# Value and output weight multiplied together ahead of the key loop, loads reordered, second key weight split inside the loop

## What is computed

```python
# first part: q is the normalised x, k = v = ctx_1024
qp = einsum('bsd,ed->bse', q, Wq) + bq
kp = einsum('bsd,ed->bse', k, Wk) + bk
vp = einsum('bsd,ed->bse', v, Wv) + bv
scores = einsum('bqd,bkd->bqk', qp, kp) * scale
attn = softmax(scores, axis=-1)
out = einsum('bqk,bkd->bqd', attn, vp)
x = x + einsum('bsd,ed->bse', out, Wo) + bo
# second part, its start
qkv = layernorm(x) @ W_qkv
q, k, v = split(qkv, 3)      # rmsnorm and relu on q and k follow
```

## Time and profile before

| | |
|---|---|
| median of 3 runs | 548.07 us (547.96 to 549.03) |
| the profiled execution | 548.39 us, span 546.3 us |
| TensorE products busy | 538.7 us, 99% of the span |
| TensorE weight loads busy | 451.8 us, 83% |
| VectorE, ScalarE, GpSimd busy | 345.9, 256.8, 197.4 us |
| first q product, first score, first product of Wv | 10.33, 34.61, 390.66 us |

### The profile page before, as it was taken

The page is one execution under the profiler, slowest core; times in us unless marked ns, Lnnn a source line. Parts: engine busy times, 40 slices in busy tenths (PEclk is TensorE's granted clock), DMA queues, the critical chain, the costliest instruction groups (busy, mean ns, idle before and its releaser), DMA issues.

```text
span 546.3 us, 7076 instructions
## 1 busy us (share of the span) xinstructions
PE 538.7 (99%) x2612; PEld 451.8 (83%) x2612; DVE 345.9 (63%) x574; ACT 256.8 (47%) x421; POOL 197.4 (36%) x125
## 2 busy tenths in 40 slices
PE   8999999999999999999999999999999999999997
PEld 7998887788888888888888888888878888888886
DVE  5745555866477655557986546998536226638757
ACT  5624346745445545454455435575355452562210
POOL 3860421312211143232212433385099709800000
PEclk9999999999999999999999999999999999999999
DMA  8602432342232224222223123423302203300002
GB/s 326 245 28 77 158 112 74 126 148 78 86 145 78 77 79 146 86 77 78 91 91 127 40 77 128 180 81 123 145 0 62 93 1 119 113 1 1 0 2 77
DMA packets 14002, 51.61 MB, mean 94 GB/s; under 512 B 1680, under 2 KB 1680, under 8 KB 13072
## 3 DMA queue, kind: packets, MB, share of 16 engines
q1 hardware_dynamic: 13968, 51.16, 26.3%
HBM read 50.11 MB, written 1.05 MB: 94 GB/s over the span
## 4 chain that ended last, share of the span: by engine, by line
PE 95%; ACT 2%; DVE 2%; issue 1%; DMA 1%; DVEq 0%
PE bank L1195 28%; PE bank L1267 11%; PE bank L1269 11%; PE bank L1268 11%; PE bank L1256 10%; PE bank L1258 10%; PE bank L1257 10%; PE bank L1185 1%; PE bank L1423 1%; DMA xs<-x 1%; PE bank L1432 0%; ACT xn L548 0%; DVE xT_l L806 0%; PE bank L1295 0%; PE bank L1551 0%
## 5 line engine op out<-in xcount | busy, mean ns | idle before, releaser
L457 POOL TENSOR_TENSOR cn_l<-raw_n,cn_h 128x1024 fp32r<-128x1024 f32 x32 | 80.1, 2502 | 207.9 <-ACT cn_h L587 207.9
L886 DVE TENSOR_TENSOR top<-top,bank 128x512 f32<-128x512 f32 x60 | 41.2, 687 | 101.1 <-ACT ring L611 100.8
L1256 PE MATMUL bank<-qk_h,ct_h 128*128 128x512 f32 x256 | 100.1, 391 | 1.1 <-DVE top L886 1.1
L1267 PE MATMUL bank<-ph,cn_h 128*128 128x512 f32 x256 | 100.4, 392 | 0.0
L1269 PE MATMUL bank<-ph,cn_l 128*128 128x512 f32 x256 | 99.7, 390 | 0.0
L1258 PE MATMUL bank<-qk_h,ct_l 128*128 128x512 f32 x256 | 99.7, 389 | 0.0
L1268 PE MATMUL bank<-pl,cn_h 128*128 128x512 f32 x256 | 99.7, 389 | 0.0
L1257 PE MATMUL bank<-qk_l,ct_h 128*128 128x512 f32 x256 | 99.7, 389 | 0.0
L611 ACT COPY ring<-bank 128x512 f32<-128x512 f32 x64 | 37.5, 586 | 75.1 <-PE bank L1258 75.1
L621 ACT ACTIVATE ph<-ring 128x512 fp32r<-128x512 f32 x64 | 40.4, 632 | 65.1 <-PE bank L1269 47.4
L913 DVE TENSOR_TENSOR ring<-ring,shift_b 128x512 f32<-128x512 f32 x64 | 60.4, 949 | 2.0 <-ACT shift_b L632 2.0
(11 more groups left out here) (213 smaller groups left out, 900.2 us busy)
## 6 DMA issues: line engine op xcount, KB each, us to landing
raw_t<-ctx_t SPq DMA_DIRECT2D x32, 512.0 KB, 4.2
raw_n<-ctx_n SPq DMA_DIRECT2D x32, 512.0 KB, 3.3
...
```

Of the source, the lines that this page charges most:

```text
L457: pool.tensor_tensor(cn[p % CNB][1][:], raw_n[p % 2][:], cn[p % CNB][0][:].bitcast(F32), ALU.subtract).then_inc(cnl_ready, 1)
L1256: pe.matmul(bank[:, dst, :], ct[i // 2 % 2][0][:, c, keys], qk[0][:, c, :], start=(c == 0), stop=False)
L1267: pe.matmul(bank[:, c, :], keys[0][:, q % 2, d], ph[q % PB][:], start=first, stop=False)
```

## The change

TensorE now computes wvo = Wv and Wo multiplied together (`fold_part`, 48 products of 512 columns) at the start, while x is loaded and normalised; its four inner chunks e follow one another over four banks, and the transposes of x stand between them. Wv, Wo and x come first on SyncE's queue, in pieces of 256 KB, and then Wq. ScalarE and VectorE split Wv and the first chunk of Wo, GpSimd the other three chunks. q and qk are computed in full width (96 products of 512 columns in place of 192 of 256). A small activation at the start (`root_table`) stands ahead of ScalarE's first cast.

In the tail the value product and the spreading of the inverse denominators are gone: the unscaled accumulator is split, one product with wvo gives y (48 products), and the scale is applied as a factor per row where y is added to x. The bias bv is carried through Wo by GpSimd (`bv_wo`, seven operations) and one plain f32 product behind score 6, and is added to bo (`y_bias`), which GpSimd adds to x as it did with bo.

The key weight of the second part (w2 k) has memory of its own now, is loaded at p = 24 and split by GpSimd behind its work on context pieces 17 and 18; the others stay in the tail, with the casts of w2 v moved on ScalarE between the applies of the LayerNorm. The one-column products for the key bias move from behind score 0 to behind score 4.

The diff, cut to its core (declarations, semaphores, memory places, the full-width q and qk evacuations, the removed value product and the split of w2 k, which is that of the other w2 weights, are left out):

```diff
-W2_ORDER = ("k", "out", "q", "v")
-W2_HIGH = {51: ("k", 0), 53: ("k", 1), 55: ("out", 0), 57: ("out", 1)}
-W2_LOW_ORDER = ("k", "q", "v", "out")
+W2_ORDER = ("out", "q", "v")
+W2_HIGH = {55: ("out", 0), 57: ("out", 1)}
+W2_LOW_ORDER = ("q", "v", "out")
+K2_SPLIT = {17: 0, 18: 1}
...
-            for t in range(0, TT, 2):
-                for n in range(t, t + 2):
-                    sp.dma_start(xs[:, n, :], x[n]).then_inc(x_loaded[n], 16)
-                for e in range(t, t + 2):
-                    sp.dma_start(wq_raw[:, e, :], wq_t[e]).then_inc(wq_loaded[e], 16)
+            def load_weights(e):
+                sp.dma_start(wv_raw[:, e, :], wv_in[e]).then_inc(wv_loaded[e], 16)
+                sp.dma_start(wo_raw[:, e, :], wo_t[e]).then_inc(wo_loaded[e], 16)
+            def load_x(t):
+                sp.dma_start(xs[:, t, :], x[t]).then_inc(x_loaded[t], 16)
+            load_weights(0)
+            load_x(0)
+            load_weights(1)
+            load_x(1)
+            load_x(2)
+            load_weights(2)
+            load_x(3)
+            load_weights(3)
+            for e in range(C):
+                sp.dma_start(wq_raw[:, e, :], wq_t[e]).then_inc(wq_loaded[e], 16)
...
-            sp.dma_start(wvo_raw[:], wv_t).then_inc(wv_loaded, 16)
...
-                if p == 6:
-                    sp.wait_ge(wvo_ready, 2)
-                    sp.dma_start(wvo_raw[:], wo_t).then_inc(wo_loaded, 16)
-                if p == NP + 3:
-                    sp.wait_ge(ctl_ready, NP)
+                if p == 24:
+                    sp.wait_ge(bo_added, TT)
                     sp.dma_start(w2_raw["k"][:], wqkv_in[1]).then_inc(w2_loaded["k"], 16)
...
+            def split_wo(e):
+                pool.wait_ge(wo_loaded[e], 16)
+                pool.tensor_copy(wo[0][:, e, :], wo_raw[:, e, :]).then_inc(wo_high, 1)
+                pool.wait_ge(wo_high, e)
+                pool.tensor_tensor(wo[1][:, e, :], wo_raw[:, e, :], wo[0][:, e, :].bitcast(F32), ALU.subtract).then_inc(wo_ready, 1)
+            pool.memset(ones[:], 1.0).then_inc(ones_ready, 1)
+            for e in range(1, C):
+                split_wo(e)
...
+            pool.wait_ge(wv_ready, C)
+            pool.wait_ge(ctl_ready, 2)
+            for e in range(C):
+                dst = bv_term if e else bv_wo
+                if e == 0:
+                    pool.wait_ge(wo_loaded[0], 16)
+                else:
+                    pool.wait_ge(bv_step, 2 * e - 1)
+                pool.tensor_scalar(dst[:], wo_raw[:, e, :], col("bv", e), None, ALU.mult).then_inc(bv_step, 1)
+                if e:
+                    pool.wait_ge(bv_step, 2 * e)
+                    pool.tensor_tensor(bv_wo[:], bv_wo[:], bv_term[:], ALU.add).then_inc(bv_step, 1)
             pool.wait_ge(xn_ready, TT)
+            pool.wait_ge(y_bias_ready, 1)
             for t in range(TT):
-                pool.tensor_tensor(xs[:, t, :], xs[:, t, :], row("bo"), ALU.add).then_inc(bo_added, 1)
-            pool.wait_ge(qk_psum, 2 * C)
...
+                if p in K2_SPLIT:
+                    split_k2(K2_SPLIT[p])
...
+            act.wait_ge(ones_ready, 1)
+            act.activation(root_table[:], ones[:], ACT.Sqrt)
+            high_wv(0)
+            act.wait_ge(wo_loaded[0], 16)
+            act.copy(wo[0][:, 0, :], wo_raw[:, 0, :]).then_inc(wo0_high, 1)
+            high_wv(1)
             std_of(0)
             apply_of(0)
+            std_of(1)
...
-            act.wait_ge(inv_psum, 1)
-            act.wait_ge(acc_scaled, (NSB - 1) * C)
-            act.copy(alpha_b[:], bank[:, MISC, :]).then_inc(invb_ready, 1)
             for c in range(C):
-                act.wait_ge(xn_ready, TT + c + 1)
+                act.wait_ge(acc_added, (NSB - 1) * C + c + 1)
                 act.copy(onT[0][:, c, :], acc[:, c, :]).then_inc(xh_ready, 1)
             for h in range(2):
                 high_w2("q", h)
-            for e in range(C):
-                act.wait_ge(v_psum, e + 1)
-                act.activation(vT[0][:, e, :], bank[:, V_BANKS[e], :], ACT.Identity,
-                               bias=col("bv", e)).then_inc(vTh_ready, 1)
-            for h in range(2):
-                high_w2("v", h)
             for t in range(TT):
                 if t >= 2:
                     high_xT(2 * TT + t - 2, X1_BANKS)
                 std_of(TT + t)
                 apply_of(TT + t)
-            act.wait_ge(w2_ready, 2 * 3)
+                if t % 2 == 0:
+                    high_w2("v", t // 2)
+            act.wait_ge(w2_ready, 2 * 2)
...
+            low_wv(0)
+            dve.wait_ge(wo0_high, 1)
+            dve.tensor_tensor(wo[1][:, 0, :], wo_raw[:, 0, :], wo[0][:, 0, :].bitcast(F32), ALU.subtract).then_inc(wo0_ready, 1)
+            low_wv(1)
             first_stats(0)
             ln_scale(0)
             first_stats(1)
             ln_scale(1)
+            low_wv(2)
             first_stats(2)
+            ln_scale(2)
             low_xT(0, XT_BANKS)
-            ln_scale(2)
+            first_stats(3)
+            low_wv(3)
+            ln_scale(3)
             low_xT(1, XT_BANKS)
-            first_stats(3)
-            ln_scale(3)
             low_xT(2, XT_BANKS)
...
+            for c in range(C):
+                dve.wait_ge(wvoh_ready, c + 1)
+                dve.tensor_tensor(wvo[1][:, c, :], bank[:, WVO_BANKS[c], :], wvo[0][:, c, :].bitcast(F32),
+                                  ALU.subtract).then_inc(wvol_ready, 1)
+            for n in range(2):
+                low_ct(n)
+            for c in range(C):
+                dve.wait_ge(qkh_ready, c + 1)
+                dve.tensor_tensor(qk[1][:, c, :], bank[:, Q_BANKS[c], :], qk[0][:, c, :].bitcast(F32),
+                                  ALU.subtract).then_inc(qkl_ready, 1)
...
+                if s == 1:
+                    sum_key_terms()
+                if s == 8:
+                    biases()
...
-                if c == 0:
-                    dve.wait_ge(invb_ready, 1)
-                dve.wait_ge(acc_added, (NSB - 1) * C + c + 1)
-                dve.tensor_tensor(acc[:, c, :], acc[:, c, :], alpha_b[:], ALU.mult).then_inc(xn_ready, 1)
                 if c > 0:
                     low_on(c - 1)
             low_on(C - 1)
-            for e in range(C):
-                dve.wait_ge(vTh_ready, e + 1)
-                dve.scalar_tensor_tensor(out=vT[1][:, e, :], in0=bank[:, V_BANKS[e], :],
-                                         scalar=col("bv", e), in1=vT[0][:, e, :].bitcast(F32), op0=ALU.add,
-                                         op1=ALU.subtract).then_inc(vTl_ready, 1)
+            dve.wait_ge(inv_ready, 1)
             dve.wait_ge(bo_added, TT)
             for t in range(TT):
                 dve.wait_ge(y_psum, t + 1)
-                dve.tensor_tensor(xs[:, t, :], xs[:, t, :], bank[:, Y_BANKS[t], :], ALU.add).then_inc(x1_ready, 1)
+                dve.scalar_tensor_tensor(out=xs[:, t, :], in0=bank[:, Y_BANKS[t], :], scalar=inv_den[:, t:t + 1],
+                                         in1=xs[:, t, :], op0=ALU.mult, op1=ALU.add).then_inc(x1_ready, 1)
...
+            def fold_part(e, c):
+                ins = project(WVO_BANKS[c], [cut(wv, e, c * P, (c + 1) * P)], [cut(wo, e, 0, D)], starts=(e == 0),
+                              stops=(e == C - 1))
+                if e == C - 1:
+                    ins.then_inc(wvo_psum, 1)
+            transposed_at = {(1, 2): 0, (2, 0): 1, (2, 2): 2, (3, 1): 3}
+            for e in range(C):
+                pe.wait_ge(wv_ready, e + 1)
+                if e == 0:
+                    pe.wait_ge(wo0_ready, 1)
+                else:
+                    pe.wait_ge(wo_ready, e)
+                for c in range(C):
+                    fold_part(e, c)
+                    if (e, c) in transposed_at:
+                        transpose_x(transposed_at[e, c])
+            pe.wait_ge(xl_ready, TT)
+            for e in range(C):
                 pe.wait_ge(wq_ready, e + 1)
-                part = slice(h * HALF, (h + 1) * HALF)
-                project(Q_BANKS[h][e], [cut(wq, e, c * P, (c + 1) * P) for c in range(C)],
-                        [cut(xT, c, part.start, part.stop) for c in range(C)], cols=part).then_inc(q_psum, 1)
-            transpose_x(0)
-            warm(KEEP_WARM)
-            transpose_x(1)
-            warm(KEEP_WARM)
-            q_half(0, 0)
-            transpose_x(2)
-            q_half(0, 1)
-            transpose_x(3)
-            q_half(0, 2)
-            q_half(0, 3)
-            for e in range(C):
-                q_half(1, e)
+                project(Q_BANKS[e], [cut(wq, e, c * P, (c + 1) * P) for c in range(C)],
+                        [cut(xT, c, 0, T) for c in range(C)]).then_inc(q_psum, 1)
             pe.wait_ge(wk_ready, 1)
...
+            for c in range(C):
+                for e in range(C):
+                    if c == 0:
+                        pe.wait_ge(qTl_ready, e + 1)
+                    if e == 0:
```

(33 more changed lines are left out.)

237 lines of the change are left out of this document (105 added, 132 removed).

## The result

The changed kernel takes **544.88 us** (median of 4 runs, 544.64 to 545.55) against 548.43 for the kernel before in the same set (547.96 to 549.03). The ratio is 0.9939, with a 95% interval of 0.9928 to 0.9951, so 3.3 us less, where 3.3 us less was forecast; the two medians themselves lie 3.55 us apart. The profiled execution took 544.86 us, span 543.1. A second set gave 544.99 us and 0.9938 (0.9926 to 0.9951), with medians 3.25 us apart.

The account below looks back on a forecast made before the run. TensorE, busy 538.7 of 546.3 us, was taken to bound the kernel. Start +7.3, bias product +1.0, score 4 +0.1 and tail -11.7 sum to -3.3 us: 544.8 for the median, range 542.6 to 547.7.

Parts of the forecast that it names:

- The start, +7.3: Start of kernel to first score: 41.9 us against 34.61, so 7.3 us later; bounds +6.0 to +9.5.
- VectorE's list: At the start: VectorE's subtractions, statistics and scales, 11.8 us without a wait from 6.7, set when q starts.
- The 1.2 us "between": At the start: VectorE waits about 1.2 us for x^T of tile 1 and 2 and for ScalarE's casts between.
- The collision term of 0.4: At the start: VectorE loses about 0.4 us behind GpSimd's wo subtractions, through shared SBUF interfaces.
- Full width, -1.2: q and qk at the start: 96 products of 512 columns take 1.2 us less than 192 halves.
- The kept-warm products "worth nothing": Old start: the kept-warm product groups between transposes lay inside waits, so dropping them costs nothing.
- rival D: Start: TensorE falls back to 1.2 GHz or has not risen, products take 0.45 us; 550.2 us, slower; chance 0.08.
- The bias product, +1.0: In the loop: the new plain f32 512-column bv row product costs 1.0 us; bounds 0.2 to 1.1.
- Score 4, +0.1: In the loop: score 4 waits for VectorE's qb sum, ct_l and peak 2, 0.1 us; bounds 0 to 0.5.
- Wk2's split, 0: In the loop: GpSimd's 6.9 us of work behind cn 17 and 18 costs 0; bounds 0 to 1.5.
- rival E: In the loop: splitting Wk2 there starves VectorE, 2 x 1.5 us lost, 547.8 us; chance 0.04.
- The tail, -11.7: Tail: first y finished 11.5 us sooner, then 0.2 less to the third projection's end; bounds -10.6 to -12.3.

Follow-up runs that it names:

- the split of the bias: Changed kernel with the plain f32 bias product made two f32r products, split by GpSimd: 546.26 us; with GpSimd's extra operations held back: 544.30 us.

## Why the prediction was right, point by point

**The start, +7.3: right in size, but the chain was another, by a hair.** The first q product came at 19.99 (20.1 forecast) and the first score at 41.87 (41.9). The sum took VectorE's list for the longest. In the changed kernel the chain that ended last was GpSimd's wo_l of part 1 and, behind it, TensorE's own order; VectorE's list ended only 0.05 us earlier, as the kernel without that wait shows (q at 19.94). So the list's length was forecast well, and that a second chain ended at the same moment, so that the number held, is luck. Nor does the list reach q without a break, as the sum had it. Its last shift is made at 16.54, and xn of tile 3 is ready at 17.6; but the transposes come at 17.98, when TensorE's order reaches them, and then a cast and a subtraction follow. VectorE was idle before the last two:

```profile
18.63 1.31 DVE L845 TENSOR_TENSOR xT_l<-bank,xT_h 128x512 fp32r<-128x512 f32 x2 [1.28 <-ACT xT_h L586]
```

The 1.2 us "between" in the sum stood for this, by luck of size. The collision term of 0.4 was a wv subtraction of 1.27 us for 0.69, 0.6.

**GpSimd's wo_l of part 1**: forecast at 8.7 to 9.2, came at 9.46, since wo1 landed at 7.1 and not 6.7 and the cast took 0.93 and not 0.6; TensorE waited 0.64, not 0.0 to 0.5. It stands on the chain that ended last, and yet only 0.05 us hung on it.

**Full width, -1.2**: right (2.0 with the wait that halves bring in the new order).

**The kept-warm products "worth nothing"**: wrong. They lay inside waits by TensorE's idle time, and yet held its clock; without them the old start loses 1.8 us. The sum did not fall with this, since it measured before's start as it was, and in the changed kernel the granted clock read 1.00 from 6 to 18 us, with fold products 0.23 apart from the second on, so rival D did not come. That the fold's products do what the kept-warm ones did is the likely reason; no kernel tested it. But the argument against D was weak. It rested on gaps of 0.4 to 0.8 us among busy stretches, and in the old start without the kept-warm products the clock fell around gaps of 1.25 and 1.43 us, with four transposes between them. The "gaps far longer than those I find" were no more than that, in a stretch that held little else.

**The bias product, +1.0**: measured 0.86. Between the product at 61.69 and that at 63.01 lie 1.32 us, of which two pitches of 0.23 are ordinary. **Score 4, +0.1**: no wait. VectorE's running maximum for it was ready at 52.46 and score 4 began at 52.75, so the margin was at most 0.3 us where 0.05 was forecast: small all the same, as the split of the bias showed. **GpSimd's bias chain** ran from 38.2 to 48.9 ("over by 48"): its multiplications took 1.57 us, just above the 0.6 to 1.5 taken. With 2 us more it would have stood over the chain to score 4, and nothing in the sum had a term for that.

**Wk2's split, 0**: right, rival E did not come. The split could as well have stayed in the tail.

**The tail, -11.7**: Y at 403.16 gives -11.5 as forecast. The 0.3 before the first k is there (Y + 7.49 for 7.35) but not for the reason named: not the cast of w2 v, but the statistics of tile 1, in line ahead of the cast of xT 0. The 0.4 before the first v is there (Y + 13.40 for 13.3) and for the reason named. The "-0.2" came out as 0.0, from these two sizes. GpSimd's slack at the last v projection was forecast as some 5 us and is 5.5:

```profile
446.06 1.04 POOL L520 CAST piece_h<-piece_raw 128x1024 fp32r<-128x1024 f32 x1 [5.50 <-PE bank L1241]
```

**What stays open.** q moved between 19.50 and 20.34 in profiles of kernels with one and the same start. Mostly it followed the end of GpSimd's wo_l of part 1, and with it the landing of wo1 and a cast of 0.61 to 1.14 us; which of the two chains comes last changes from profile to profile, and effects on the start below 0.5 us can't be told from this. No kernel had the fold without the new load order and the old tail, so the fold's own price and return are known from the stages alone.
